# Cross-attention and quantised FFN in float32: where the queries of the last three batches are turned

## The reference

```
q      = layernorm(x)                                  # 512 x 512 a batch
scores = q @ context.T / sqrt(512), masked entries -1e9
p      = softmax(scores)
x1     = x + (swap(p @ context) @ W_merge.T + b_merge) # swap: rows and columns of the product
xq     = fake_quant(layernorm(x1), one scale over all batches)
h      = fake_quant(silu(xq @ Wg.T) * (xq @ Wu.T), one scale over all batches)
out    = x1 + h @ Wd.T                                 # Wg, Wu, Wd rounded to 8 bits by row
```

## Time and profile before

| | |
|---|---|
| median of 3 runs | 533.05 us (531.87 to 533.37) |
| profiled execution | 532.62 us |
| its span | 530.8 us |
| busy over the span: TensorE, VectorE, ScalarE, GpSimd | 524.1, 437.2, 301.7, 151.1 us |
| granted TensorE clock | 1.00 |
| DMA: moved, share of 16 engines' span | 93.61 MB, 63.8% (SP's queue) |

### The profile page before, as it was taken

How to read it: one execution, slowest core, us unless ns; L and a number is a source line. 1 busy time by engine, 2 the same in 40 slices (tenths; PEclk the granted TensorE clock), 3 DMA queues, 4 the chain that set the end, 5 groups by cost and what they waited for, 6 DMA issues and landing times. The chain is left out here.

```text
span 530.8 us, 7462 instructions
## 1 busy us (share of the span) xinstructions
PE 524.1 (99%) x2497; PEld 349.0 (66%) x2497; DVE 437.2 (82%) x821; ACT 301.7 (57%) x455; POOL 151.1 (28%) x101
## 2 busy tenths in 40 slices
PE   7999999999999999999999999999999999999997
PEld 7888888888888888888888444444444445444444
DVE  5798999969699698896668688778878787699985
ACT  4695866657647565575333754654654533977620
POOL 3369556556457553674131000000000000000000
PEclk9999999999999999999999999999999999999999
DMA  8927579795884857942478639677301100879785
GB/s 276 294 73 162 183 176 150 248 189 183 204 148 188 195 171 188 157 160 84 110 80 186 237 68 309 232 187 254 110 9 40 40 1 27 332 260 383 270 274 217
DMA packets 77888, 93.61 MB, mean 176 GB/s; under 512 B 36128, under 2 KB 54944, under 8 KB 75296
## 3 DMA queue, kind: packets, MB, share of 16 engines
q1 hardware_dynamic: 77712, 93.15, 63.8%
q10 hardware_dynamic: 144, 0.07, 0.0%
HBM read 59.77 MB, written 25.43 MB: 161 GB/s over the span
## 5 line engine op out<-in xcount | busy, mean ns | idle before, releaser
L1467 PE MATMUL gu<-hid,gu_T 128*128 128x512 f16 x496 | 111.1, 379 | 0.0
L1467 PEld LDWEIGHTS gu<-hid,gu_T 128*128 128x128 f16 x496 | 48.5, 98 | 58.6
L1234 ACT ACTIVATE hid<-gu,gu_mul 128x512 f32<-128x512 f32 x63 | 43.2, 685 | 54.1 <-PE gu L1467 47.1
L1333 DVE SCALAR_TENSOR_TENSOR hid<-gu,gu_mul,hid 128x512 f32 (+1 forms) x63 | 47.0, 747 | 28.6 <-PE gu L1467 16.9
L1349 DVE TENSOR_REDUCE hmax<-hid 128x1 f32 (+2 forms) x48 | 52.7, 1109 | 1.3 <-DVE hid L1333 1.3
L1272 ACT ACTIVATE h<-hid,inv 128x512 int8<-128x512 f32 (+3 forms) x35 | 44.3, 1343 | 11.7 <-DVE gu_T L1386 11.7
L456 ACT ACTIVATE probs<-probs,nmax 128x512 f32<-128x512 f32 x32 | 23.0, 720 | 45.7 <-DVE nmax L640 45.7
L910 PE MATMUL mm<-cT_hi,qT_hi 128*128 128x512 f32 x124 | 48.8, 394 | 0.0
L912 PE MATMUL mm<-cT_hi,qT_lo 128*128 128x512 f32 x124 | 48.3, 390 | 0.0
L911 PE MATMUL mm<-cT_lo,qT_hi 128*128 128x512 f32 x124 | 48.3, 390 | 0.0
L912 PE MATMUL mm<-g_hi,c_lo 128*128 128x512 f32 x124 | 48.3, 390 | 0.0
(11 more groups left out here) (193 smaller groups left out, 1047.7 us busy)
## 6 DMA issues: line engine op xcount, KB each, us to landing
h_dram<-hid SPq DMA_DIRECT2D x3, 2816.0 KB, 9.3
hid<-h_dram SPq DMA_DIRECT2D x3, 2816.0 KB, 11.5
cb<-in_ctx_dram SPq DMA_DIRECT2D x28, 256.0 KB, 7.7
cx<-in_ctx_dram SPq DMA_DIRECT2D x7, 1024.0 KB, 11.0
x<-in_x_dram SPq DMA_DIRECT2D x5, 1024.0 KB, 7.4
x_dram<-x SPq DMA_DIRECT2D x20, 256.0 KB, 2.4
xq<-x_dram SPq DMA_DIRECT2D x5, 1024.0 KB, 10.4
x<-x_dram SPq DMA_DIRECT2D x5, 1024.0 KB, 4.9
```

What stands on the lines that cost most here:

```text
L1234: nc.scalar.activation(silu[SILU_AT[i]], gu[2 * (i % 3)][:], ACT.Silu, scale=gu_mul[:, 0, i:i + 1]).then_inc(silu_done, 1)
L1333: nc.vector.scalar_tensor_tensor(hid[:, b % SLOTS, i * L:(i + 1) * L], gu[2 * (i % 3) + 1][:], gu_mul[:, 1, i:i + 1], silu[SILU_AT[i]], AL ...
L1467: last = nc.tensor.matmul(gu[2 * (i % 3) + g][:], gu_T[:, g, h, i * P:(i + 1) * P], xT[p][:, h, :], start=h == 0, stop=h == T - 1)
```

## The change

For batches 5, 6 and 7 (`BLOCK_Q`) the queries no longer go through TensorE. `norm1` writes them in plain column order. SP stores each tile in rows to a new DRAM tensor and reads it back with four DMAs of 32 partitions each (64 KB, runs of 512 bytes), so that VectorE's transpose of 32 x 32 blocks completes it, in place in `qn`. ScalarE and VectorE then make the high and low parts from SBUF. SP does this after the weight loads of the batch and ahead of the x1 stores. VectorE's turns stand behind `mixed_lo(n, 1)` (tiles 0 and 1) and `mixed_lo(n, 2)` (tiles 2 and 3); the splits of tiles 0, 1 stand ahead of the third mixed tile, those of tiles 2, 3 ahead of the fourth. The scores wait for `q_split`.

```diff
+    BLOCK_Q = range(B - 3, B)
+    q_dram = nc.dram_tensor("q_dram", (len(BLOCK_Q), L, D), F32, kind="Internal").ap()
...
                 def turned_ahead(n, k):
-                    if n == B - 1:
+                    if n + 1 in BLOCK_Q or n == B - 1:
                         return ()
                     return (k,) if n == 1 else range(T) if k == T // 2 else ()
+                def block_queries(n):
+                    return T * (n - BLOCK_Q[0])
...
+                HALF_ROWS = (range(T // 2), range(T // 2, T))
...
+                    def queries_out(n, t):
+                        sp.wait_ge(q_ready, T * n + t + 1)
+                        sp.dma_start(q_dram[n - BLOCK_Q[0], t * P:(t + 1) * P, :], qn[:, t, :]).then_inc(q_out[t], 16)
+                    def queries_back(n, t):
+                        pieces = q_dram[n - BLOCK_Q[0], t * P:(t + 1) * P, :].rearrange("(k j) (a f) -> a j k f", j=BLK, f=P)
+                        sp.wait_ge(q_out[t], 16 * (n - BLOCK_Q[0] + 1))
+                        for a in range(P // BLK):
+                            sp.dma_start(qn[a * BLK:(a + 1) * BLK, t, :].rearrange("j (k f) -> j k f", f=P),
+                                         pieces[a]).then_inc(q_back[t], 16)
+                    def queries_by_blocks(n):
+                        for t in range(T - 1):
+                            queries_out(n, t)
+                        queries_back(n, 0)
+                        queries_out(n, T - 1)
+                        for t in range(1, T):
+                            queries_back(n, t)
...
                             load_w(n)
+                            if n + 1 in BLOCK_Q:
+                                queries_by_blocks(n + 1)
                             for t in range(T):
                                 store_x1(n - 1, t)
...
+                    def block_query_hi(n, t):
+                        act.wait_ge(q_turned, block_queries(n) + t + 1)
+                        if t == 0:
+                            act.wait_ge(s_done, T * n)
+                        nc.scalar.activation(columns(qT_hi, t), blocks(qn[:, t, :]), ACT.Copy).then_inc(q_hid, 1)
...
                         if n and t == 0:
-                            act.wait_ge(t_done, T * (n + 1))
+                            if n - 1 in BLOCK_Q:
+                                act.wait_ge(q_split, block_queries(n))
+                            else:
+                                act.wait_ge(t_done, T * (n + 1))
                         q, x_row = qn[:, t, :], xs[n % 3][:, t, :]
-                        if n:
+                        if n and n not in BLOCK_Q:
...
                                 for g in turned_ahead(n, k):
                                     transposed_hi(n + 1, T + g)
+                                if n + 1 in BLOCK_Q and k >= T // 2:
+                                    for t in HALF_ROWS[k - T // 2]:
+                                        block_query_hi(n + 1, t)
                                 mixed_hi(n, k)
...
+                    def block_query_turn(n, t):
+                        dve.wait_ge(q_back[t], 64 * (n - BLOCK_Q[0] + 1))
+                        nc.vector.transpose(qn[:, t, :], qn[:, t, :]).then_inc(q_turned, 1)
+                    def block_query_lo(n, t):
+                        dve.wait_ge(q_hid, block_queries(n) + t + 1)
+                        nc.vector.tensor_tensor(columns(qT_lo, t), blocks(qn[:, t, :]), columns(qT_hi, t).bitcast(F32),
+                                                ALU.subtract).then_inc(q_split, 1)
...
                                 for g in turned_ahead(n, k):
                                     transposed_lo(n + 1, T + g)
+                                if n + 1 in BLOCK_Q and k >= T // 2:
+                                    for t in HALF_ROWS[k - T // 2]:
+                                        block_query_lo(n + 1, t)
                                 mixed_lo(n, k)
+                                if n + 1 in BLOCK_Q and 1 <= k <= T // 2:
+                                    for t in HALF_ROWS[k - 1]:
+                                        block_query_turn(n + 1, t)
...
-                        pe.wait_ge(t_lo, turns(n, T + k) if n else max(turns(0, T + k), turns(0, T - 1)))
+                        if n in BLOCK_Q:
+                            pe.wait_ge(q_split, block_queries(n) + k + 1)
+                        else:
+                            pe.wait_ge(t_lo, turns(n, T + k) if n else max(turns(0, T + k), turns(0, T - 1)))
```

More of the change, by code:

```diff
@@ L153, in attention @@
                 t_done, t_hi, t_lo = sem("t_done"), sem("t_hi"), sem("t_lo")
+                q_out, q_back = [sem(f"q_out{t}") for t in range(T)], [sem(f"q_back{t}") for t in range(T)]
+                q_turned, q_hid, q_split = sem("q_turned"), sem("q_hid"), sem("q_split")
                 wm_done, wm_hid, wm_ready = sem("wm_done"), sem("wm_hid"), sem("wm_ready")
```

## The result

The changed kernel takes 539.27 us (median of 4 runs, 538.61 to 539.68); the kernel before, run beside it, 532.92 (4 runs, 531.87 to 533.37). The ratio is 1.0129 with a 95% interval of 1.0113 to 1.0144: 6.4 us slower, where 1.7 faster was forecast; the range, to 534.0, doesn't hold it. One run of the kernel before, 540.49 us beside e5 to e8, was in a slower state of the chip and is left out of their ratios.

What follows compares the result with a forecast made beforehand. TensorE, busy 34.41 of 34.41 us a batch, was taken to bound the attention stage. Terms: -5.3 (transposes) + 2.9 (query waits) + 0.75 (reload in the tail) = -1.7 us; forecast 531.3 us, range 530.0 to 534.0.

Steps and rivals of the forecast that it cites:

- stops: TensorE idle before the scores of batches 6 and 7, waiting for split queries: about 1.1 and 1.8 us.
- The subtraction from SBUF: VectorE's query subtraction, now reading SBUF: 0.68 us taken, between 0.68 from below and 0.88 from above.
- its chain: VectorE's turns and subtractions until TensorE may start: 3.27 us behind the anchor, the start of the first mixed low parts.
- rival (b): VectorE lags more, 0.5 us a batch in two batches: gain about 0.7 us, time 532.4; chance 0.26.
- (a): The full gain of 5.3 us, 527.7 us, with VectorE delivering queries 3 us earlier in batch 6; chance 0.04.
- The transfers: Query round trip through SP's queue: 0.4 us to issue a piece, about 3 to land, stores landing after 2.4.
- hidden: Batch 4's round trip lands before VectorE wants it: tiles 0 and 1 by 169 for 171.85, tile 3 by 172 for 175.6.
- x is loaded at 172.5: x for batch 6, behind the x1 stores on SP's queue: loaded about 172.5, landed by 180, wanted at 183.3.
- the blocks of the context and the context itself: Later loads on SP's queue: move by the same 4 us and are wanted later still.
- Rival (c): Late round trip at tile 3's turn, deciding from 0.66 us an issue: 3 x 1.4 = 4.2 us, about 535.5; chance 0.15.
- The tail: After batch 7, TensorE's turns of batch 0's reread rows wait for the reload, giving back 0.75 us.

Runs made afterwards that it cites:

- e5: e4 with the four x1 stores put between the queries' transfers as VectorE finishes them; 532.72 us, ratio 1.0002.
- e8: Kernel before, with the x1 stores of batches 3 to 5 held in SP's queue about as late as the change makes them, no bytes added; 532.62 us.
- e1: Changed kernel without the store and reload of the queries, turns waiting only for the normalised rows; 531.06 us, ratio 0.9976.
- e4: Changed kernel with queries returned in 8 transfers of 128 KB a batch instead of 16 of 64 KB; 540.11 us, ratio 1.0134.
- e11: Changed kernel with blocks for the last two batches only, in e5's order and halves; 532.30 us, ratio 1.0000.
- e6: Changed kernel with blocks for the queries of batch 7 only; 530.52 us (10 runs), ratio 0.9953.
- e13: e6 with the tail's reload of batch 0's rows moved ahead of the last weight scale's store; 530.94 us, ratio 0.997.
- e3: Changed kernel with 32 extra matmuls on constants ahead of the scores of batch 7; 539.73 us, ratio 1.0134.
- e7: Changed kernel with pieces read to a second DRAM tensor instead of back, turns waiting only for the stores; 542.24 us, ratio 1.0179.
- e10: Changed kernel, 16 pieces a batch kept, with only the x1 stores put between the queries' transfers; 534.72 us, ratio 1.0046.
- e12: e11 with e13's edit, the tail's reload ahead of the last scale's store; 534.09 us, ratio 1.0028.
- e14: Changed kernel with batch 7's four query stores issued by ScalarE instead of SP; 539.11 us, ratio 1.0128.

## Why the prediction was wrong

**TensorE and VectorE: right.** Batch 5's scores at 174.57 (174.56 forecast), batch 6's at 208.55 (208.3), stops of 1.18 and, in e1, 1.51 (1.1 and 1.8). e1 is the forecast's sum without its transfers, and its median is 1.8 us under before's beside it (1.7 forecast). That this agrees so well is in part luck: its interval holds no change too, and its trace gains 0.7 us from batch 4 to the end. The subtraction from SBUF took 0.69 us in batch 5 (0.68 taken). VectorE was busy 31.4 and 30.9 us in batches 5 and 6, less than the 32.2 to 32.4 worked out, and its chain held, so rival (b) did not come; nor did (a).

**The transfers: the step that failed.** The piece's issue was right (0.43 us against 0.4), and its landing was shorter than taken (1.9 to 2.3 us, against 3). The store's landing, taken from the median of 2.4, held in batch 4 only (2.0 to 2.3): tile 0's took 5.7 us in batch 5 and 6.7 in batch 6, where it was issued close behind the weight loads. In batch 4 queries were "hidden", as worked. The failure is in what was read off from this one batch and taken for all three: that x is loaded at 172.5 (175.63 measured: the x1 stores had to be issued and to land behind the twelve last pieces), and above all "the blocks of the context and the context itself move by the same 4 us and are wanted later still". That asks when VectorE wants them, not what they run beside. They run beside the weight turns, which then take 11.1 and 10.3 us to land instead of 5.4 and 6.3; SP waits for these, and behind it stand the next batch's weights and the next batch's own query stores. The chain closes on itself: weights 3.8 late in batch 5 (191.97 against 188.15), 9.4 in batch 6. That there was little room was to be seen in the trace of before: between the context's load and the weight turns SP had 8.0 us free in batch 4 (173.80 to 181.79) and 5.4 in batch 5 (211.00 to 216.42, a scale's store in it), while the trip moved x by 7.1 us (175.63 for 168.56) and then by 11.5 (214.51 for 203.02).

**Rival (c): right in sign, wrong in place.** It priced the round trip at tile 3 by the issue of a piece (from 0.66 us on). The pieces cost 0.43 and e4, with half as many, was no better; the late ones were tiles 0 and 1, through the order. It gave +4.2 before the 1.7 came off; by the table the scores of batch 7 came 6.7 us later than forecast (107.46 against 100.8), and the clock took 2.7 on top.

**The tail.** 0.75 was forecast to be given back to the reload. e1 gives back 0.36 there (47.17 us from the scores to the next phase against before's 46.82) and 1.28 at the next phase's first products, which wasn't foreseen. In e11 the reload takes 2.4. In e6 and e13 it takes nothing. The term depends on when SP issues the reload (130.6 us behind the scores of batch 4 in e6, 132.4 in e11), not on TensorE's lead alone.

**The clock.** No part of the forecast, as no stop was over 1.8 us. It took 2.7 us in the trace; e3 kept it up and gained nothing in its median, for reasons that are only in part known. e7 shows that 1.8 us needn't be safe: behind a stop of 1.82 the clock did fall.

Open: how the 9.4 us split between bytes and order (e8 has 4.6 with x 6.0 us late and no bytes added), what makes the 2.0 us between e10 and e5, and e12.

## What to carry to other kernels

A transfer put into an in-order queue must be followed past its own landing: list what stands behind it, what those transfers will now run beside, which wait of the issuing engine that stretches, and whether the next round of the new transfer stands behind this wait. Work it through for the second and third round, not the first alone. Where a change repeats per batch, try it in the last one, where no load of a next x and no further trip follows it in the queue: here that part alone is worth having (530.5 us), and the two batches ahead of it, in the order of the change, cost 8.7 us more.

## What the runs showed of the hardware

- DMA transposes beside ordinary loads land later and cost SP more time. With the context's blocks and the context (2 MB) still moving they took 11.1 and 10.3 us to land, against 5.4 and 6.3 before and 3.9 and 3.6 in e6; in e8 late loads alone gave 11.0 and 10.8. The one at L322 took 4.15 us to issue instead of 1.48. The wait behind them before the next weights could be loaded was 5.6 us (229.12 to 234.68) against 4.1 (221.24 to 225.29), but it was 1.35 in e6, so that this part of the cost is less certain.
- A 256 KB store landed 2.0 us after its issue on a quiet queue and 6.7 right behind 1 MB of loads. From another engine's queue, issued ahead of those loads but beside transposes in flight, it took 7.1 (e14), and the loads were later by 2.6.
- TensorE's clock: stops of 1.2 to 1.5 us left it at the 2.4 GHz level (e1, e5). Behind stops of 1.82 and 2.13 us it fell 1.3 to 1.5 us after work began again (e7), behind 2.67 us after 0.9, for 3.4 us (e12), behind 3.11 at once for 2.7 (e10), behind 7.52 at once for 5.6 (after).
- A piece of 64 KB from DRAM to DRAM took about 0.6 us to issue (e7), from DRAM to SBUF 0.43.
